# Three reorderings in a five-pass graph kernel: norm scalings, first attention rows, a third projection bank

## The reference

```python
x = _layernorm(x + _L0_gnn_ref(x, adj, adj, Wq, Wk, Wv, bv, Wo, bo))   # attention, 12 heads, bias 2*adj
x = _layernorm(x + _L1_gnn_ref(x, adj, Wq, bq, Wk, bk, Wv, bv, beta))  # attention, masked where adj <= 0, no Wo
x = _layernorm(x + _L2_gnn_ref(x, adj, Wl, bl, Ws, bs, Wr, br, ln_w, ln_b))
x = _layernorm(x + _L3_gnn_ref(x, adj, Wq, Wk, Wv, bv, Wo, bo))        # attention, 12 heads, bias adj
```

```python
u = jnp.einsum('bid,bjd->bij', h, h) / temper
delta = jax.nn.softmax(u, axis=-1) * adjacency_matrix
attn = delta / (jnp.sum(delta, axis=-1, keepdims=True) + 1e-10)
hl, hs, hr = h @ wl.T + b_l, h @ ws.T + b_s, h @ wr.T + b_r
ctx = einsum(attn * upper, hl) + diag_a[..., None] * hs + einsum(attn * lower, hr)
h = relu((ctx - mean) / jnp.sqrt(var + LN_EPS) * g + beta)
```

## Time and profile before

| what | value |
|---|---|
| median of three runs | 2798.38 us |
| the profiled execution: its time, its span | 2798.66 us, 2796.7 us |
| TensorE matmuls busy | 2603.2 us (93%) |
| VectorE busy | 2019.2 us (72%) |
| GpSimd busy | 1807.4 us (65%) |
| ScalarE busy | 1563.3 us (56%) |
| mean granted clock of TensorE | 0.976 |

### The profile page before, as it was taken

One profiled execution on the slowest core, in us unless ns is written; L12 is line 12 of the kernel. 1 busy time (PEld: TensorE's weight loads), 2 busy tenths in 40 slices (PEclk: granted clock), 3 DMA queues, 4 the chain that ended last, 5 costly groups with the idle time before them and its releaser, 6 DMA issues. The chain is left out here.

```text
span 2796.7 us, 66048 instructions
## 1 busy us (share of the span) xinstructions
PE 2603.2 (93%) x22686; PEld 2220.3 (79%) x22686; DVE 2019.2 (72%) x3473; ACT 1563.3 (56%) x3192; POOL 1807.4 (65%) x2045
## 2 busy tenths in 40 slices
PE   7999999987999999869999979999997899999997
PEld 6888888875777777668888868777775788888886
DVE  4888888874888888746666655677776488888887
ACT  4555555544565555545656646666665555555553
POOL 2777777772666666646666646777776377777776
PEclk9999999998999999979999989999998999999999
DMA  3222222112222222132122122222222212222211
GB/s 107 71 71 69 68 68 68 57 47 84 73 79 84 75 74 76 51 97 73 58 65 68 57 76 85 92 81 80 91 80 66 66 59 67 68 71 68 68 57 49
DMA packets 179196, 200.52 MB, mean 72 GB/s; under 512 B 56580, under 2 KB 179080, under 8 KB 179080
## 3 DMA queue, kind: packets, MB, share of 16 engines
q1 hardware_dynamic: 179080, 198.99, 22.9%
HBM read 136.03 MB, written 62.91 MB: 71 GB/s over the span
## 5 line engine op out<-in xcount | busy, mean ns | idle before, releaser
L1099 PE MATMUL l_ps_h<-l_w,l_hT 128*128 128x384 f32 x3456 | 680.5, 344 | 22.6 <-ACT l_hlr L1193 22.0
L418 PE MATMUL l_ps_p<-l_xT,l_w 128*128 128x512 f32 x2592 | 678.1, 406 | 16.8 <-ACT l_qT L559 8.7
L1099 PEld LDWEIGHTS l_ps_h<-l_w,l_hT 128*128 128x128 f32 x3456 | 595.8, 189 | 75.0 <-issue 40.7
L418 PEld LDWEIGHTS l_ps_p<-l_xT,l_w 128*128 128x128 f32 x2592 | 468.2, 189 | 123.7 <-ACT l_qT L559 16.1
L345 POOL TENSOR_TENSOR l_pr<-l_sc,l_st 128x768 f32<-128x768 f32 x192 | 283.4, 1476 | 389.9 <-DVE l_st L693 389.9
L315 POOL TENSOR_TENSOR v<-v,l_bvs 128x768 f32<-128x768 f32 x192 | 376.0, 1958 | 0.0
L412 PE MATMUL l_ps_p<-l_w,l_xT 128*128 128x384 f32 x1728 | 341.9, 344 | 21.2 <-ACT l_k L565 17.7
L578 ACT ACTIVATE v<-l_ps_p 64x192 f32<-64x192 f32 x768 | 250.1, 326 | 175.2 <-PE l_ps_p L412 168.0
L1010 POOL TENSOR_TENSOR l_hlr<-l_hlr,l_sides 128x768 f32<-128x768 f32 x128 | 239.6, 1872 | 167.0 <-ACT l_hlr L1193 167.0
L700 DVE TENSOR_REDUCE l_st<-l_pr 128x12 f32<-128x768 f32 x192 | 182.8, 952 | 202.5 <-ACT l_pr L611 200.4
L412 PEld LDWEIGHTS l_ps_p<-l_w,l_xT 128*128 128x128 f32 x1728 | 294.7, 188 | 29.6 <-ACT l_k L565 21.2
(11 more groups left out here) (127 smaller groups left out, 4369.4 us busy)
## 6 DMA issues: line engine op xcount, KB each, us to landing
rows<-l_yo SPq DMA_DIRECT2D x256, 192.0 KB, 1.9
l_xa<-rows SPq DMA_DIRECT2D x64, 768.0 KB, 5.0
l_xr<-rows SPq DMA_DIRECT2D x192, 192.0 KB, 2.4
l_xa<-in_x SPq DMA_DIRECT2D x16, 768.0 KB, 5.0
l_xr<-in_x SPq DMA_DIRECT2D x64, 192.0 KB, 2.4
out<-l_yo SPq DMA_DIRECT2D x64, 192.0 KB, 1.9
l_edge<-in_adj SPq DMA_DIRECT2D x80, 128.0 KB, 2.4
raw<-in_L_gnn_Wq SPq DMA_DIRECT2D x3, 576.0 KB, 6.1
```

What stands on the lines that cost most here:

```text
L418: last = nc.tensor.matmul(bank[:, :], W[m][:, l, t, o * P:(o + 1) * P], rows[:, r, t, :], start=c + t == 0, stop=c == 2 and t == KT - 1)
L1099: last = nc.tensor.matmul(ps_h[m][:, :D], hT[gpar][:, l, t, s * P:(s + 1) * P], W[m][:, r, t, :], start=c + t == 0, stop=m != SELF and c = ...
```

## The change

It has three parts.

1. In `digcn_pass`, ScalarE's `standardise(n - 2)` and `normed(n - 4)` move from ahead of the RIGHT copy to behind it (and behind the row copies that follow it in the first unit).
2. In `digcn_pass`, TensorE's `attention_T(0)` moves from ahead of the loop to behind the first unit's SELF projection, and ScalarE's copy of its result, `attention(0, 0, 2)`, to behind the first unit's SELF copy.
3. In `attention_pass`, where there is no output projection (pass two), pieces take three banks, `ps_p0`, `ps_p1` and `ps_y`, by the table `THIRD`; the wait is for the last user of the same bank.

```diff
+        THIRD = (0, 1, 2, 0, 1, 2, 0, 1, 2, 0, 1, 2, 1)
+
         def bank_of(par, pos):
-            return ps_p[(par + pos) % 2]
+            return ps_p[(par + pos) % 2] if wo else (*ps_p, ps_y)[THIRD[pos]]
 
         def user_before(i, pos):
 
+            bank = THIRD[pos]
             while True:
-                pos -= 2
+                pos -= 2 if wo else 1
                 if pos < 0:
                     i, pos = i - 1, pos + len(AHEAD)
+                if not wo and THIRD[pos] != bank:
+                    continue
                 if exists(i, pos) or isinstance(i, int) and i < -1:
                     return i, AHEAD[pos]
...
             pe.wait_ge(c_zero, zeros)
-            attention_T(0)
             pe.wait_ge(c_row, rows_ready)
...
                     if s == 0:
                         rows_T(i + 1, 1 - par, (2,))
+                    if isinstance(n, int) and n == 0:
+                        attention_T(0)
                     if s == 3:
                         attention_T(i + 1)
...
             rows_T(0, 0)
-            for step in range(1, 3):
-                attention(0, 0, step)
+            attention(0, 0, 1)
...
-                    standardise(n - 2, b)
-                    normed(n - 4, pair * 4 + 2 * par + s // 2 - 2, b)
                     left_right(n, b, RIGHT)
                     if s == 0:
                         rows_T(i + 1, 1 - par, (1,))
+                    standardise(n - 2, b)
+                    normed(n - 4, pair * 4 + 2 * par + s // 2 - 2, b)
                     relu(n - 2, pair * 4 + 2 * par + s // 2 - 1, b)
...
+                    if isinstance(n, int) and n == 0:
+                        attention(0, 0, 2)
                     if s == 0:
                         rows_T(i + 1, 1 - par, (2,))
```

## The result

The changed kernel took 2717.51 us in the median of four runs (2715.76 to 2721.26), the kernel before 2798.12 beside it: ratio 0.9715, 95% interval 0.9698 to 0.9732, 80.6 us less. The forecast was 2721.5.

What follows compares the result with a forecast made beforehand. TensorE was taken to wait for other engines in passes two to four. Gains of 42 + 12 + 23 = 77 us took 2798.66 to 2721.7, or 2721.5 on the runs' scale; the 8 in 10 range was 2704 to 2749.

Steps and rivals of the forecast that it cites:

- Reading by pass, pass three as yardstick: Passes three and four run the same TensorE programme, so pass four's 456.37 against 412.75 us means 43.6 lost to other engines.
- the ring of 6.05 us: Pass four: GpSimd's addition, inner statistics, both scalings and the right copy wait on each other, 6.05 us a unit.
- The cover of the scalings: Pass four: behind the right copy the scalings delay nothing, since the SELF copy waits for its matmuls anyway; cost nothing.
- the slower rival: Pass four's ring still closes in one unit, with SELF copy and VectorE's sum: 102 us more there, total 2865; chance 0.04.
- two us lost at the widened rows: Pass four, third unit of a group: VectorE's rows up to 0.3 us late in 14 groups, 4 us, half taken.
- the two cases: Pass four, VectorE and GpSimd port lock: gain 44 us if the addition follows VectorE's multiplication, 40 if it comes first.
- Part 2, 12 us: Starts of passes three and four: first projection 5.4 us earlier, transposes cost 0.4, clock adds; 6 us a pass.
- The sixth, for the clock: Starts of passes three and four: a clock gain beyond the 5.0 us, bringing each pass to 6 us.
- Part 3, 23 us: Pass two: a third bank removes waits for key and query copies; 15 groups at 1.43 us make 21, prologue 2.
- The ring of VectorE and GpSimd: Pass two: logits, maximum, subtraction, bias and residual additions, statistics limit a group to 31.4 us: 9.34 plus 22.05.
- The prologue: Start of pass two, where only TensorE works: two places of about 1.2 and 0.6 us, taken as 2 us.
- the transposes of the exponentials: Pass two: where TensorE would wait once VectorE and GpSimd fall behind it by a us in each group.

Runs made afterwards that it cites:

- e1: The kernel before with only ScalarE's two norm scalings moved behind the RIGHT copy in pass four: 2754.02 us against 2798.51.
- e7: The kernel before with only the outer norm's scaling moved behind the RIGHT copy in pass four: 2759.3 us against 2796.26.
- e8: The kernel before with only the inner norm's scaling moved behind the RIGHT copy in pass four: 2797.87 us against 2796.26.
- e9: The changed kernel with each norm scaling of pass four run a second time, result unread: 2721.71 us against 2797.36 for the kernel before.
- e3_bank: The kernel before with only the third projection bank in pass two: 2774.73 us against 2798.51.
- e6_both: The changed kernel, in pass two with tile load ahead of store and residual addition ahead of value bias: 2693.88 us, ratio 0.9635 to the kernel before.

## Why the prediction was right

- **Reading by pass, pass three as yardstick: right.** Pass four lost 43.6 us to other engines, and part 1 gave back exactly these (e1: 456.4 to 412.75).
- **Part 1, the ring of 6.05 us: right.** Shown by e7 and e8: the outer scaling closes it, the inner one alone frees nothing. The cover of the scalings that I took as free holds twice their time (e9). That also removes the slower rival: the SELF copy is not on the path. (Its price was off too: the copy takes 0.58 us and VectorE's sum 0.56, not 0.7 and 0.9.)
- **Part 1, two us lost at the widened rows: the one mis-sized term.** It is 0. Of the two cases that I gave for the rule of the Trainium skill on the shared ports ("SBUF — State Buffer", section "SBUF: two separate sides"), 44 and 40, the first came: in the new rhythm the addition comes after the multiplication, and 0.43 us in place of 1.91 made the chain shorter by more than was missing. The gain's multiplication above agrees with the rule as well: where it begins inside an addition, its end follows the addition's by 0.41 to 0.44 us.
- **Part 2, 12 us: right in size** (11.3 in the profile, 12.7 by the medians). The projection starts 2.76 us after the products instead of 8.19, 5.4 earlier, and the transposes take 0.4 of it back; that is 5.0 of the 6 us a pass. The sixth, for the clock, no run shows as a fixed term. In the changed kernel's profile most of it came in pass four (first projection 2.39 instead of 3.23) and none in pass three's first projection, which took 3.25 as before and had the clock at 0.50 from 1192 to 1196 although TensorE was busy throughout. That the sum still came to 12 is in part luck. Over the six profiles with part 2 pass three's start took 13.6 to 14.9 us, over the seven without 19.4 to 20.3.
- **Part 3, 23 us: right** (25.1 in the profile, 23.8 alone). The ring of VectorE and GpSimd gives 31.43 us a group for 31.4 forecast, and its units measure what I had added up: 9.34 for the third (9.34 forecast), 7.4 for the others (7.35). The prologue gave 3 us (40.61 to 37.55 us from the pass's first transposes to the second input tile that the first group turns) for the 2 I took. Where the wait would be seen was wrong: I named the transposes of the exponentials, and it stood at the input tile, because SyncE's queue passes VectorE's lateness on to the tile.
- The sum, 77, was 3.6 us short of the 80.6 measured: 2 of it the widened rows, 1 the prologue of pass two, the rest within what pass one and pass two vary between executions.

## What to carry to other kernels

A wait is worth what the ring it belongs to can still lose: write down every member of the ring, durations and hand-overs, and count how many units it spans; the instruction that waits for the last thing in the ring has to move (37 of 44 us here), and moving only its neighbour gives nothing. Once a resource (here the third bank) is freed, look for the next ring in the same stretch at once, and expect several of nearly the same length, of which one alone pays little. A transfer that an engine waits for may be late only because it stands in a queue behind something that this engine's partner makes.

## What the runs showed that I had not expected

A wait of two us for an input tile was at times followed by a loss of its own. In e9_twice_after, in pass two, where it equals the changed kernel:

```profile
801.02 0.66 PE L388 MATMUL l_ps_p<-ident,l_xa 128*128 128x128 f32 x4 [2.04 <-DMA l_xa<-rows]
801.44 3.57 PE L423 MATMUL l_ps_y<-l_xT,l_w 128*128 128x512 f32 x9
```

Behind the wait the projection took 3.57 us instead of 2.35, and the granted clock of that stretch was 0.65:

```profile
801.00:805.00 4.00, 3.98 (x17) 2.77 (x18) 2.77 (x6) 1.33 (x2) 3.04 (x4) 0.65 0.13 49
```

VectorE then waited 1.39 us for the logits, and the group took 33.9 us. The same came twice more in that execution (waits of 2.11 and 2.39 us, projections of 3.41 and 3.46) and once in e3_bank's (1.98, then 3.33); in the changed kernel's profile one wait was as long, 2.06 us up to 799.16, and the clock stayed at 1.00 behind it:

```profile
801.00:805.00 4.00, 4.00 (x62) 3.17 (x62) 3.59 (x8) 1.48 (x3) 1.86 (x4) 1.00 0.19 53
```

With 0, 1 and 3 such places the profiles of the changed kernel, e3_bank and e9_twice_after have pass two at 547.4, 549.5 and 553.1 us, while e6_both, without any wait, repeats its 30.13 us in thirteen groups. What decides whether the clock falls behind such a wait stays open.
